# A mixture-of-experts and scan block on one core: its opening rearranged, and the hand-written order of all engines shifted with it

## What is computed

```python
x = x + 0.5 * ffn(layernorm(x))
x = x + mixer(layernorm(x))
x = x + 0.5 * ffn(layernorm(x))

# ffn, for each batch b of 1024 tokens, 8 experts, the best 2 taken
logits = z.mean(axis=1) @ gate_w             # one routing per batch
w, e = top_k(softmax(logits), 2); w = w / w.sum()
out = sum(w[k] * (gelu(z @ w1[e[k]] + b1[e[k]]) @ w2[e[k]] + b2[e[k]]) for k in (0, 1))
```

## Time and profile before

| | us |
|---|---|
| median of 3 runs | 274.96 (274.55 to 275.35) |
| profiled execution | 275.18, its span 273.4 |
| PE busy | 255.6 (93%) |
| DVE busy | 222.6 (81%) |
| ACT busy | 207.2 (76%) |
| POOL busy | 45.6 (17%) |
| mean DMA rate | 52 GB/s |
| granted clock, mean | 0.997 |

### The profile page before, as it was taken

The page is one execution under the profiler, slowest core; times in us unless marked ns, Lnnn a source line. Parts: engine busy times, 40 slices in busy tenths (PEclk is TensorE's granted clock), DMA queues, the critical chain, the costliest instruction groups (busy, mean ns, idle before and its releaser), DMA issues.

```text
span 273.4 us, 3572 instructions
## 1 busy us (share of the span) xinstructions
PE 255.6 (93%) x1056; PEld 177.2 (65%) x1056; DVE 222.6 (81%) x567; ACT 207.2 (76%) x254; POOL 45.6 (17%) x58
## 2 busy tenths in 40 slices
PE   0899999999999989999999999997999999999994
PEld 0796676665656656666566566564777778778781
DVE  3569578559999999999999999999999997546252
ACT  1069584558998959969889979889996697689462
POOL 5320200430006002533006151003000030000000
PEclk9999999999999999999999999999999999999998
...
GB/s 208 140 174 135 103 54 0 0 74 84 1 0 0 2 73 82 1 2 0 151 5 0 2 2 154 0 0 2 0 0 2 157 0 0 224 86 0 0 0 153
DMA packets 13762, 14.17 MB, mean 52 GB/s; under 512 B 1008, under 2 KB 9456, under 8 KB 13744
## 3 DMA queue, kind: packets, MB, share of 16 engines
...
q10 hardware_dynamic: 672, 0.27, 0.4%
...
...
## 4 chain that ended last, share of the span: by engine, by line
PE 72%; ACT 8%; DVE 8%; issue 7%; DMA 3%; SPq 1%; POOL 0%; ACTq 0%; DVEq 0%; POOLq 0%
PE y_ps L684 32%; PE hid_ps L655 25%; PE aux_ps L752 3%; PE aux_ps L708 3%; PE aux_ps L784 3%; PE aux_ps L733 2%; PE aux_ps L773 2%; ACT vb L558 2%; PE y_ps L792 1%; DMA xt<-x_dram 1%; DVE hid_lo L931 1%; ACT dt_t L547 1%; DMA w_sb<-wpack_dram 1%; ACT hid L475 1%; ACT yt L504 1%
## 5 line engine op out<-in xcount | busy, mean ns | idle before, releaser
L475 ACT ACTIVATE hid<-hid_ps,w_sb 128x1024 f32<-128x1024 f32 x64 | 70.2, 1108 | 19.9 <-PE hid_ps L655 19.6
L684 PE MATMUL y_ps<-hid,w_sb 128*128 128x512 f32 x168 | 79.2, 594 | 0.0
L655 PE MATMUL hid_ps<-z_hi,w_hi 128*128 128x512 f32 x128 | 51.6, 484 | 0.8 <-ACT hid L475 0.8
L684 PEld LDWEIGHTS y_ps<-hid,w_sb 128*128 128x128 f32 x168 | 30.8, 190 | 22.9 <-issue 20.3
L931 DVE TENSOR_TENSOR hid_lo<-hid,hid_hi 128x1024 fp32r<-128x1024 f32 x22 | 26.6, 1222 | 19.8 <-ACT hid_hi L482 19.8
L655 PE MATMUL hid_ps<-z_lo,w_hi 128*128 128x512 f32 x128 | 39.9, 393 | 0.0
L655 PE MATMUL hid_ps<-z_hi,w_lo 128*128 128x512 f32 x128 | 39.8, 392 | 0.0
L655 PEld LDWEIGHTS hid_ps<-z_hi,w_hi 128*128 128x128 f32 x128 | 23.1, 189 | 16.1 <-issue 12.4
L655 PEld LDWEIGHTS hid_ps<-z_hi,w_lo 128*128 128x128 f32 x128 | 24.0, 188 | 5.5
L655 PEld LDWEIGHTS hid_ps<-z_lo,w_hi 128*128 128x128 f32 x128 | 24.0, 188 | 5.5
L482 ACT ACTIVATE hid_hi<-hid 128x1024 fp32r<-128x1024 f32 x22 | 22.7, 1055 | 1.5 <-PE y_ps L684 1.4
...
## 6 DMA issues: line engine op xcount, KB each, us to landing
...
rope_sb<-rope_dram POOLq DMA_DIRECT2D x1, 1024.0 KB, 7.9
...
```

What stands on the lines that cost most here:

```text
L475: nc.scalar.activation(hid[:, slot % HBUF, :], hid_ps[:, slot % 2, :], ACT.Gelu, bias=bias).then_inc(hid_ready, 1)
L655: last = nc.tensor.matmul(hid_ps[:, slot % 2, cols], w, z[:, q % 2, cols], start=first, stop=end)
L684: last = nc.tensor.matmul(y_ps[:, cols], wt, src[:, cols], start=t == 0 and i == 0, stop=t == SLOTS - 1 and end)
```

## The change

- x[0] comes in four transfers of two tiles, two on SyncE's queue, two on ScalarE's; the statistics wait for each pair.
- The first 256 columns (`HEADS` = 2 blocks) of w1 of all eight experts are loaded at the start, into `w_heads`, which shares its memory with the later `state` and `gated`. When the index is known, ScalarE and DVE each read it into a register and split these columns from there (`split_heads`); SyncE no longer issues the head of expert 1, and the rest of its w1 starts at column 256. The mixer's first writers of `state` and `gated` wait for the splits.
- rope moves from GpSimd's queue to SyncE's, behind x[3]. The `in_chunk` memset on GpSimd moves ahead of its first power.
- PE turns the normalised tiles first, in two halves; ScalarE copies each half and sums it (`accum_out`), DVE widens the sum of both, and then PE makes the logits. The eight summing matmuls are gone. 13 dummy matmuls stand before the turns, 5 behind the logits in place of 14.
- ScalarE runs turn_z(0) (with its z_hi copy) ahead of read_logits(0). DVE runs split_z, split_heads and coefficients ahead of the statistics of pass 1.
- The ticks of `up`, `gelu` and `down` rise by 40, and all places of `AT` are new, most of them by some 40 too, but with changes of order.

```diff
-DOWN = {False: 58, True: 92}
+DOWN = {False: 98, True: 132}
...
-        "f_norm": {1: 86, 2: 389, 3: 709, 4: 1029, 5: 1369, 6: 1686, 7: 2046},
-        "f_route": {1: 135, 2: 429, 3: 849, 4: 1109, 5: 1429, 6: 1775, 7: 2086},
-        "m_norm": {0: 469, 1: 809, 2: 1129, 3: 1469},
-        "m_dt": {0: 609, 1: 909, 2: 1249, 3: 1606},
-        "m_v": {0: 629, 1: 929, 2: 1269, 3: 1612},
-        "m_heads": {0: 886, 1: 1189, 2: 1549, 3: 1884},
-        "m_out": {0: 892, 1: 1229, 2: 1589, 3: 1888},
+        "f_norm": {1: 126, 2: 306, 3: 749, 4: 1069, 5: 1409, 6: 1766, 7: 2126},
+        "f_route": {1: 189, 2: 389, 3: 809, 4: 1109, 5: 1449, 6: 1884, 7: 2149},
+        "m_norm": {0: 529, 1: 869, 2: 1189, 3: 1509},
+        "m_dt": {0: 669, 1: 969, 2: 1309, 3: 1629},
+        "m_v": {0: 689, 1: 1009, 2: 1329, 3: 1649},
+        "m_heads": {0: 945, 1: 1269, 2: 1606, 3: 1926},
+        "m_out": {0: 952, 1: 1289, 2: 1612, 3: 1946},
...
-        "c_mixer": {0: 316},
+        "c_mixer": {0: 285},
-        "f_stats": {2: 152, 3: 348, 4: 914, 5: 1254, 6: 1610, 7: 1946},
+        "f_stats": {2: 166, 3: 319, 4: 976, 5: 1320, 6: 1652, 7: 2043},
-        "f_split_z": {1: 129, 2: 615, 3: 772, 4: 1271, 5: 1537, 6: 1890, 7: 2084},
+        "f_split_z": {1: 184, 2: 363, 3: 813, 4: 1148, 5: 1596, 6: 1952, 7: 2200},
-        "f_normalise": {2: 298, 3: 624, 4: 976, 5: 1338, 6: 1654, 7: 2025},
+        "f_normalise": {2: 194, 3: 464, 4: 1033, 5: 1380, 6: 1758, 7: 2109},
-        "f_route": {1: 148, 2: 476, 3: 881, 4: 1161, 5: 1452, 6: 1888, 7: 2095},
+        "f_route": {1: 246, 2: 458, 3: 847, 4: 1162, 5: 1553, 6: 1927, 7: 2212},
-        "m_stats": {0: 387, 1: 710, 2: 1033, 3: 1382},
+        "m_stats": {0: 433, 1: 760, 2: 1082, 3: 1420},
-        "m_decay": {0: 636, 1: 945, 2: 1278, 3: 1629},
+        "m_decay": {0: 701, 1: 1009, 2: 1345, 3: 1670},
-        "m_scan2": {0: 847, 1: 1167, 2: 1502, 3: 1864},
+        "m_scan2": {0: 899, 1: 1221, 2: 1558, 3: 1906},
...
-        "f_turn": {1: 72, 2: 380, 3: 700, 4: 1020, 5: 1380, 6: 1710, 7: 2024},
+        "f_turn": {1: 140, 2: 340, 3: 740, 4: 1060, 5: 1386, 6: 1780, 7: 2130},
-        "m_scale": {0: 453, 1: 786, 2: 1130, 3: 1432},
+        "m_scale": {0: 533, 1: 860, 2: 1173, 3: 1500},
-        "m_tap": {0: 466, 1: 826, 2: 1150, 3: 1493},
+        "m_tap": {0: 546, 1: 885, 2: 1210, 3: 1526},
-        "f_split_w1": {1: 230, 2: 493, 3: 900, 4: 1184, 5: 1526, 6: 1910, 7: 2133},
+        "f_split_w1": {1: 300, 2: 620, 3: 902, 4: 1186, 5: 1553, 6: 1946, 7: 2230},
...
-    WARM = 14
+    WARM_EARLY, WARM = 13, 5
+    HEADS = 2
...
+        late = sb("late", [P, 2, N])
+        state, gated = late[:, 0, :], late[:, 1, :]
+        w_heads = late[:, :, :].rearrange("p a n -> p (a n)").rearrange("p (e n) -> p e n", e=E)
...
-                    head = P if q == 0 and k == 0 else 0
-                    if head:
-                        sp.dma_start(w_sb[:, 0, 0, 0:head], src[k][:, 0:head]).then_inc(w1_head_in, 16)
+                    head = HEADS * P if q == 0 and k == 0 else 0
                     sp.dma_start(w_sb[:, q % 2, k, head:W2_AT], src[k][:, head:W2_AT]).then_inc(w1_in[q % 2][k], 16)
...
-            sp.dma_start(xt[:, 0, 0:NT // 2, :], x0[:, 0:NT // 2, :]).then_inc(x_in[0], 16)
+            for i in range(2):
+                sp.dma_start(xt[:, 0, 2 * i:2 * i + 2, :], x0[:, 2 * i:2 * i + 2, :]).then_inc(x0_in[i], 16)
             sp.dma_start(gate_sb[:, :], gate_w).then_inc(small_in, 16)
+            sp.dma_start(w_heads[:, :, :], wpack[:, :, 0:HEADS * P].rearrange("e p n -> p e n")).then_inc(w_heads_in, 16)
             load_x(1)
             load_experts(0)
             load_x(2)
             load_x(3)
+            sp.dma_start(rope_sb[:, :, :], rope.rearrange("k p n -> p k n")).then_inc(rope_in, 16)
...
+            nc.gpsimd.memset(in_chunk[:, :], 1.0).then_inc(made_const, 1)
+            pool.wait_ge(made_const, 7)
+            nc.gpsimd.memset(first_of(in_chunk), 0.0).then_inc(made_const, 1)
             pool.dma_start(proj_sb[:, :, :], proj.rearrange("p (k n) -> p k n", n=P)).then_inc(proj_in, 16)
-            pool.dma_start(rope_sb[:, :, :], rope.rearrange("k p n -> p k n")).then_inc(rope_in, 16)
...
             def turn_z(q):
 
-                act.wait_ge(f_turned, q + 1)
                 if q:
+                    act.wait_ge(f_turned, q + 1)
                     act.wait_ge(zwide_ready, q)
                 f_feat = f_tok[:, :, :].rearrange("p t d -> p (t d)")
-                nc.scalar.activation(f_feat, aux_ps[:, :], ACT.Copy, accum_out=zsum[:, :]).then_inc(zt_ready, 1)
+                if q == 0:
+                    act.wait_ge(f_turned_head, 1)
+                    nc.scalar.activation(f_feat[:, 0:HALF], aux_ps[:, 0:HALF], ACT.Copy,
+                                         accum_out=zsum[:, 0:1]).then_inc(zt_head, 1)
+                    act.wait_ge(f_turned, 1)
+                    nc.scalar.activation(f_feat[:, HALF:], aux_ps[:, HALF:], ACT.Copy,
+                                         accum_out=zsum[:, 1:2]).then_inc(zt_ready, 1)
+                    act.wait_ge(zt_head, 1)
+                else:
+                    nc.scalar.activation(f_feat, aux_ps[:, :], ACT.Copy, accum_out=zsum[:, 0:1]).then_inc(zt_ready, 1)
                 act.wait_ge(zt_ready, q + 1)
...
+            def split_heads():
+
+                act.wait_ge(w_heads_in, 16)
+                act.wait_ge(index_ready, 1)
+                first = act.value_load(top_i[0:1, 0:1], min_val=0, max_val=E - 1)
+                for f in range(HEADS):
+                    rows = slice(f * P, (f + 1) * P)
+                    nc.scalar.activation(w1_hi[:, 0, 0, rows],
+                                         w_heads[:, bass.ds(first, 1), rows].rearrange("p e n -> p (e n)"),
+                                         ACT.Copy).then_inc(w1_head_hi, 1)
 
...
-            act.dma_start(xt[:, 0, NT // 2:, :], x0[:, NT // 2:, :]).then_inc(x_in_tail, 16)
+            for i in range(2, 4):
+                act.dma_start(xt[:, 0, 2 * i:2 * i + 2, :], x0[:, 2 * i:2 * i + 2, :]).then_inc(x0_in[i], 16)
             act.dma_start(vec_sb[:, :], vecs).then_inc(vecs_in, 16)
             nc.scalar.preload_act_table_set("gelu_and_others")
+            turn_z(0)
             read_logits(0)
-            turn_z(0)
+            split_heads()
             top_tanh(0)
             split_w1(0)
             act.wait_ge(vecs_in, 16)
             act.wait_ge(made_const, 6)
             at = AT["act"]
             for tick in range(LAST):
-                for slot in slot_at(tick, 0):
+                for slot in slot_at(tick, TICKS):
...
-                if slot == 0:
-                    pe.wait_ge(w1_head_hi, 1)
-                elif slot == 1 or f == 0:
+                if slot < HEADS:
+                    pe.wait_ge(w1_head_hi, slot + 1)
+                elif slot == HEADS or f == 0:
...
-            for t in range(NT):
-                pe.wait_ge(f_norm_done, t + 1)
-                last = nc.tensor.matmul(y_ps[:, 0:P], f_tok[:, t, :], ones[:, :], start=t == 0, stop=t == NT - 1)
-            last.then_inc(zwide_up, 1)
+            for _ in range(WARM_EARLY):
+                nc.tensor.matmul(hid_ps[:, 0, 0:P], ones[:, :], ones[:, :], start=True, stop=True)
+            pe.wait_ge(made_ident, 2)
+            pre_norm(0)
             pe.wait_ge(small_in, 16)
             pe.wait_ge(zwide_ready, 1)
             nc.tensor.matmul(y_ps[:, HALF:HALF + E], zsum_wide[:, :], gate_sb[:, :],
                              start=True, stop=True).then_inc(logits_up, 1)
-            pe.wait_ge(made_ident, 2)
-            pre_norm(0)
 
             for _ in range(WARM):
...
+            def split_heads():
+
+                dve.wait_ge(index_ready, 1)
+                first = dve.value_load(top_i[0:1, 0:1], min_val=0, max_val=E - 1)
+                for f in range(HEADS):
+                    rows = slice(f * P, (f + 1) * P)
+                    dve.wait_ge(w1_head_hi, f + 1)
+                    V.tensor_tensor(w1_lo[:, 0, 0, rows],
+                                    w_heads[:, bass.ds(first, 1), rows].rearrange("p e n -> p (e n)"),
+                                    w1_hi[:, 0, 0, rows].bitcast(F32), ALU.subtract).then_inc(w1_head_lo, 1)
 
             def widen_sum(q):
                 dve.wait_ge(zt_ready, q + 1)
                 if q:
                     dve.wait_ge(logits_up, q)
-                V.tensor_scalar(zsum_wide[:, :], ones[:, :], zsum[:, 0:1], None, ALU.mult).then_inc(zwide_ready, 1)
+                    V.tensor_scalar(zsum_wide[:, :], ones[:, :], zsum[:, 0:1], None, ALU.mult).then_inc(zwide_ready, 1)
+                else:
+                    dve.wait_ge(zt_head, 1)
+                    V.tensor_scalar(zsum_wide[:, :], ones[:, :], zsum[:, 0:1], zsum[:, 1:2],
+                                    ALU.mult, ALU.add).then_inc(zwide_ready, 1)
...
             pass_normalise(0)
-            dve.wait_ge(zwide_up, 1)
```

(7 more changed lines are left out.)

149 lines of the change are left out of this document (74 added, 75 removed), and 6 rows, old and new, of the table AT.

## The result

The change made the kernel slower. The changed kernel takes 276.18 us, the median of 6 runs (276.04 to 276.71), the kernel before, beside it, 275.12 (274.49 to 275.59): ratio 1.0044, 95% interval [1.0027, 1.0061]. The forecast was 274.6. The time lies inside the range, but on the other side of no change. The profiled execution took 276.16 us with a span of 274.3, close to the median.

The account below looks back on a forecast made before the run. PE taken to bound 30 to 47 us and after 211, DVE 73.2 to 211.0, a chain the opening. From 275.18: -1.75 + 1.45 + 0.2 - 0.5 + 0.2 = -0.4, so 274.8; median 0.2 lower, 274.6; range 272.3 to 276.8.

Parts of the forecast that it names:

- x in four transfers, the memset: Opening: second pair of x tiles 0.55 us sooner, memset moved into GpSimd's wait saves 0.41; last normalised tile at 9.0.
- One expert transfer fewer: Opening: without the head, expert 2's w1 transfer goes 0.5 us sooner after the index; it lands 1.75 sooner, at 17.4.
- The early first up is worth nothing on the chain: Opening: first up starts 4.6 us sooner, but gelu(0) stands behind split_w1(0), which waits for both experts; no gain.
- The new order up to m_decay.0: Opening's end to batch 0's m_decay: rearranged tables start it 1.45 us later relative to PE, only 0.3 sooner overall.
- The first term: Ahead of batch 0's y update: pass 2's transposes (0.88) and route (0.17) delay its mixer 1.05 us relative to PE's work.
- The second, up12 and gelu12 ahead of batch 0's first steps: Ahead of m_norm.0 and m_scale.0: batch 0's transposes come 1.39 us later; of gelu12's 1.10, 0.25 shows behind them.
- From m_decay.0 to the last scan: DVE-bound stretch: same 135.4 us of DVE work in both orders, new holes +0.2 us, bounds -1.1 to +2.
- DVE gets holes: DVE-bound stretch: m_norm.1 and m_norm.2 behind one more down make DVE wait, +1.7 us, 276.3; chance 0.12.
- The rival on the clock: PE falls to 1.2 GHz in its hole before up(2), slowing up(2), pre_norm(1), down0: +1.6 us, 276.2; chance 0.14.
- Gain passes: Mixer's first chain not lengthened by up12 and gelu12, so m_decay starts the full 1.75 us sooner: 273.0; chance 0.28.
- Behind the last scan: After 211 us, PE-bound: order heads, down45, out, up48 saves 0.5 us; pass 7's later route costs 0.2.

Follow-up runs that it names:

- o4: e1 with x[0] in two transfers and the in_chunk memset behind GpSimd's powers again: 273.98 us, ratio 0.9945.
- v1: e1 with expert 1's work first: first two gelus ahead of the second expert's split, third up ahead of down0: 271.65 us, ratio 0.9891.
- e1: Changed kernel with the order tables of the kernel before, every tick raised by 40: 273.18 us, ratio 0.9923.
- o1: e1 with 14 dummy matmuls instead of 5 ahead of the first up: 273.65 us, ratio 0.9934.
- e5: Changed kernel with batch 0's m_norm, m_scale and m_tap put ahead of pass 3's chunk 12: 276.87 us, ratio 1.0057.
- v2: v1 with split_z(0) ahead of pass 1's statistics again on DVE: 272.04 us, ratio 0.9868.

## Why the prediction was right or wrong, step by step

**x in four transfers, the memset.** Index predicted 12.0, measured 11.95. The parts were 0.33 (0.55 predicted) and 0.40 (0.41), by o4, so something else in the chain was a little cheaper than I had it.

**One expert transfer fewer.** The second expert's w1 was issued at 14.06 instead of 15.89, 1.83 sooner (1.75 predicted). It landed at 16.79, not 17.4, since the same transfer took 2.73 us where the earlier trace rows has 3.26. I had kept its duration constant while I moved 1024 KB of other traffic around it. This 0.53 is most of the 0.56 us by which the opening was mis-sized, to the good. That the other traffic is the reason is my reading; no run takes it alone, and the 64 KB head that stood in front of the transfer is gone as well.

**The early first up is worth nothing on the chain.** The hole was there (1.84 us), and v1, which fills it, is 1.5 us faster than e1: right, apart from o1's open half us.

**The new order up to m_decay.0.** +1.45 predicted, +1.35 measured. The first term, 1.05 of PE work ahead of the y update, is as the traces have it (1.04 by the marks, the start at 46.18 against 45.08 in e1). The second, up12 and gelu12 ahead of batch 0's first steps, did move the clip of `xs`, and e5 took 0.8 of that back; but m_decay.0 did not follow, and e5 lost 0.7. The prediction carried the delay through silu as one chain; in the trace silu waits behind a gelu that PE's work sets. So the sum was right here and the path in it was not, and that part is luck.

**From m_decay.0 to the last scan.** Here the prediction failed. I compared the sets of DVE's steps, found them equal, and took the holes as +0.2 with +2 as the upper bound. Equal sets were right (306 instructions, 135.3 us in both), but the term was mis-sized by 2.0 us: the bound, not the value, came true. What I did not do was to look at what waits on the other side of DVE's queue: the earlier trace rows already had DVE waiting 2.67 us for m_inv in batch 0, and for the later batches the slack of that wait (0.2 to 0.8 us, fill less chain, in the table) was to be had from the trace of before. The clip and the difference beside the two m_var steps make the chain 0.9 to 1.5 longer, and the slack is gone. The price per step was hinted at as well: one of the m_var steps of before took 0.67, beside a clip, where the other two took 0.20.

**The rival "DVE gets holes"** named the right side, place and size (276.3 against 276.18), but another cause, m_norm behind one more `down`; no hole there was found. That its time is so near is in part luck: the holes cost 2.05 more than the sum had, and the opening gave 0.56 more.

**The rival on the clock** did not decide the changed kernel: the clock fell, in the dummies and the first `up`, where the hole behind covers it, and the transposes of pass 1 ran at full pace (1.04 at 20.05). The hole of 1.84 us did not lower it either: 1.00 from 16 to 22 us. The Trainium skill, "TensorE: Matmul & The Clock Gate", section "Why this matters for your kernels", warns of idle gaps; the trace has the clock lower only ahead of that hole, at 0.65 and 0.78 between 10 and 16 us. v1 and v2 have no such cover, and in v2's profiled execution down0's third product comes 2.07 us later than in v1's (24.75 against 22.68); how much of that the clock takes is not parted from their other difference, the place of split_z(0).

**"Gain passes"** did not come about: 0.96 of 2.31 us reached m_decay.0.

**Behind the last scan.** -0.3 predicted, -0.4 measured.
